# Key/value projections as seven block products (Strassen–Winograd) instead of eight

## The reference, cut to what matters

```python
q = rms_norm((x @ Wq).reshape(b, 32, 32, 128))
k = rms_norm((ctx @ Wk).reshape(b, 512, 8, 128))      # ctx is the same for both layers
v = (ctx @ Wv).reshape(b, 512, 8, 128)
probs = softmax(q @ k.T / sqrt(128))                  # 4 query heads share a key head
out = (probs @ v).reshape(b, 32, 4096) @ Wo
```

## Time and profile before

| | value |
|---|---|
| runs | 1511.18 us median, 1509.8 to 1514.25 |
| profiled execution: span | 1508.9 us; the median of the runs is 2.3 us above it |
| PE busy | 99% |
| DVE, ACT, POOL busy | 58%, 49%, 21% |
| granted TensorE clock | 0.999 of 2.4 GHz |
| chain that ended last | PE 94%, DVE 3%, ACT 1%, issue 1% |
| DMA | 99.37 MB, 66 GB/s on the mean |

### The profile page before, as it was taken

The page is one execution under the profiler, slowest core; times in us unless marked ns, Lnnn a source line. Parts: engine busy times, 40 slices in busy tenths (PEclk is TensorE's granted clock), DMA queues, the critical chain, the costliest instruction groups (busy, mean ns, idle before and its releaser), DMA issues.

```text
span 1508.9 us, 23714 instructions
## 1 busy us (share of the span) xinstructions
PE 1490.3 (99%) x8326; PEld 1269.7 (84%) x8326; DVE 876.7 (58%) x1645; ACT 733.5 (49%) x1360; POOL 311.5 (21%) x494
## 2 busy tenths in 40 slices
PE   8999999999999999999999999999999999999998
PEld 6888888888888888889778888888888888887887
DVE  6845554555555455758667555455554545577665
ACT  5634444545445454646456444444444444563443
POOL 2322221212222121014233222212222222101000
PEclk9999999999999999999999999999999999999999
DMA  8110000000000001447071000000000000252242
GB/s 326 53 66 30 17 27 19 19 26 12 35 16 26 19 20 62 147 170 258 29 279 60 22 8 28 7 21 21 7 28 7 21 14 15 93 187 91 85 167 98
DMA packets 29306, 99.37 MB, mean 66 GB/s; under 512 B 7040, under 2 KB 7808, under 8 KB 23648
## 3 DMA queue, kind: packets, MB, share of 16 engines
q1 hardware_dynamic: 29248, 98.60, 18.3%
HBM read 95.83 MB, written 2.75 MB: 65 GB/s over the span
## 4 chain that ended last, share of the span: by engine, by line
PE 94%; DVE 3%; ACT 1%; issue 1%; POOL 0%; DMA 0%; SPq 0%; DVEq 0%; POOLq 0%; ACTq 0%
PE g_kbanks L54 10%; PE g_kbanks L56 10%; PE g_kbanks L55 10%; PE g_vbank L54 9%; PE g_vbank L55 9%; PE g_vbank L56 9%; PE g_pobanks L1490 7%; PE g_pobanks L1478 4%; PE g_ktbank L1502 4%; PE g_sbank L1468 3%; PE g_sbank L54 2%; PE g_sbank L56 2%; PE g_sbank L55 2%; PE g_pobanks L54 1%; PE g_pobanks L56 1%; PE g_pobanks L55 1%
## 5 line engine op out<-in xcount | busy, mean ns | idle before, releaser
L54 PE MATMUL g_kbanks<-c_wkv_lo_r,c_cT_hi 128*128 128x512 f32 x640 | 262.5, 410 | 1.9 <-DVE c_wkv_lo_r L339 1.0
L56 PE MATMUL g_kbanks<-c_wkv_hi,c_cT_lo_r 128*128 128x512 f32 x640 | 250.4, 391 | 0.0
L55 PE MATMUL g_kbanks<-c_wkv_hi,c_cT_hi 128*128 128x512 f32 x640 | 249.8, 390 | 0.0
L54 PE MATMUL g_vbank<-c_wkv_lo_r,c_cT_hi 128*128 128x512 f32 x512 | 200.4, 391 | 0.0
L55 PE MATMUL g_vbank<-c_wkv_hi,c_cT_hi 128*128 128x512 f32 x512 | 200.0, 391 | 0.0
L56 PE MATMUL g_vbank<-c_wkv_hi,c_cT_lo_r 128*128 128x512 f32 x512 | 199.8, 390 | 0.0
L56 PEld LDWEIGHTS g_kbanks<-c_wkv_hi,c_cT_lo_r 128*128 128x128 f32 x640 | 120.1, 188 | 26.4
L54 PEld LDWEIGHTS g_kbanks<-c_wkv_lo_r,c_cT_hi 128*128 128x128 f32 x640 | 120.5, 188 | 24.7 <-issue 3.8
L55 PEld LDWEIGHTS g_kbanks<-c_wkv_hi,c_cT_hi 128*128 128x128 f32 x640 | 120.8, 189 | 20.7
L56 PEld LDWEIGHTS g_vbank<-c_wkv_hi,c_cT_lo_r 128*128 128x128 f32 x512 | 96.1, 188 | 20.6
L54 PEld LDWEIGHTS g_vbank<-c_wkv_lo_r,c_cT_hi 128*128 128x128 f32 x512 | 96.2, 188 | 18.5
(11 more groups left out here) (538 smaller groups left out, 3562.1 us busy)
## 6 DMA issues: line engine op xcount, KB each, us to landing
c_cT_lo<-in_ctx SPq DMA_DIRECT2D x64, 256.0 KB, 2.5
c_wkv_lo<-in_l_wo SPq DMA_DIRECT2D x16, 1024.0 KB, 4.8
g_stage<-in_l_wq SPq DMA_DIRECT2D x15, 1024.0 KB, 5.2
e_stage<-in_e_w SPq DMA_DIRECT2D x20, 768.0 KB, 4.1
c_wkv_lo<-in_l_wkv SPq DMA_DIRECT2D x8, 1024.0 KB, 7.5
m_stage<-in_mix_ffn SPq DMA_DIRECT2D x10, 768.0 KB, 4.6
c_vlat<-vlat_dram SPq DMA_DIRECT2D x32, 64.0 KB, 1.8
m_tw_lo<-in_mix_out SPq DMA_DIRECT2D x1, 1792.0 KB, 7.2
```

The source lines that it names most:

```text
L54: nc.tensor.matmul(out, a[0], b[1], start=start, stop=False)
L55: nc.tensor.matmul(out, a[0], b[0], start=False, stop=False)
L56: return nc.tensor.matmul(out, a[1], b[0], start=False, stop=stop)
```

## The change

Two key tiles and both columns (K and V) make a 2×2 block problem with an inner size cut in two: context blocks A11, A12, A21, A22 and weight blocks B11, B12, B21, B22. It was eight block products (48 matmuls for two key tiles); now seven (42), by sums of blocks made before. A product is 6 matmuls. The loop body is a **quad**: two key tiles, of which there are 32 in a layer, numbered m.

What goes with it:
- **Order of units**: all batches with the first half of heads, then all batches with the second, since seven weight blocks of one half fill the room. Halfway the weights are "turned": 4 POOL differences, 7 ACT and 7 DVE splits of 1024 columns (`turned_sum`, `turned_hi`, `turned_lo`).
- **Context blocks**: seven per pair of tiles, S1 to S4 made by POOL (4 operations of 256 columns), split by ACT and DVE in two pieces (768 and 1024 columns). This is done once, in the first half of the first layer. Each result (1.8 MB) is stored to DRAM, and fetched from there in all later units (48 fetches of 1.8 MB in two pieces).
- **Results**: the seven products end in two key banks and the value bank; ACT copies P1, P1-side partial sums (U2, U3) out, and DVE adds three times per quad.
- **Latents** of the first layer pass through the stream of query weights; their keys go through DRAM.
- The probabilities' 32 extra rows move from the score bank to the transpose bank.
- In the last quad two pieces of the output and four of the output weights are split.

```diff
-def mm3(nc, out, a, b, start, stop):
+def mm3(nc, out, a, b, start, stop, reopen=False):
...
+        def product(side, left, right, bank, start):
+            a, wt = context.block(side, left), kvw.block(right)
+            for c in range(DC // 2):
+                last = mm3(nc, bank[:, :], tuple(h[:, c * P:(c + 1) * P] for h in a),
+                           tuple(h[:, c * UW:(c + 1) * UW] for h in wt),
+                           start and c == 0, c == DC // 2 - 1, not start)
+            return last
...
+        def quad(hf, b, par, cycle, u, side, m):          # PE
...
+            need(pe, ka_added, m)
+            product(side, context.A11, kvw.B11, x_bank, True).then_inc(products, 1)
+            need(pe, k_normed, 2 * m)
+            product(side, context.A12, kvw.B21, y_bank, True).then_inc(products, 1)
+            if lags(u, side):
+                pv(a - 1, 1 - par if side else par, (2 * side - 1) % UNIT_H)
+            kt(2 * m - 1, 1, a if on else 0)
+            pe.wait_ge(p1_kept, m + 1)
+            product(side, context.S2, kvw.T2, x_bank, False).then_inc(products, 1)
+            need(pe, va_added, m)
+            product(side, context.S1, kvw.T1, zbank, True).then_inc(products, 1)
+            score(a, 1 - par, 2 * side)
+            pe.wait_ge(u2_kept, m + 1)
+            product(side, context.S3, kvw.T3, x_bank, False).then_inc(products, 1)
+            kt(2 * m, 0, a)
+            score(a + 1, 1 - par, 2 * side + 1)
+            pe.wait_ge(u3_kept, m + 1)
+            product(side, context.A22, kvw.T4, x_bank, False).then_inc(products, 1)
+            p_transpose(a, 2 * side, 2 * m + 1)
+            pe.wait_ge(vb_added, m + 1)
+            product(side, context.S4, kvw.B22, zbank, False).then_inc(products, 1)
+            pv(a, 1 - par, 2 * side)
+            p_transpose(a + 1, 2 * side + 1, 2 * m + 1)
...
+        def quad(hf, b, par, cycle, u, side, m):          # POOL
+            if prepared(hf, m + 1):
+                context.sums(pool, *following(hf, b, side))
+            if side == 1:
+                split_queries(u, par, 2 * m)
+            else:
+                root(2 * m, 0)
+            if is_at(m, PAIRS // 2 - 1):
+                pool.wait_ge(products, made(m, "p5"))
+                kvw.turned_sum(pool, 0)
+                pool.wait_ge(products, made(m, "p6"))
+                kvw.turned_sum(pool, 1)
+                pool.wait_ge(products, made(m, "p4"))
+                kvw.turned_sum(pool, 2)
+            root(2 * m + 1, 1)
+            if is_at(m, PAIRS // 2 - 1):
+                kvw.turned_sum(pool, 3)
```

More of the change, by code:

```diff
@@ L387, in product @@
         for h in range(GROUP):
-            last = mm3(self.nc, self.ybank[t], tuple(half[:, q % self.RING, h * P:(h + 1) * P] for half in self.split),
+            last = mm3(self.nc, self.ybank[t],
+                       tuple(self.context.slot(half, q % self.RING)[:, h * P:(h + 1) * P] for half in range(2)),
                        tuple(half[:, h * D:(h + 1) * D] for half in wt),
@@ L533, in gpsimd @@
                                     ALU.pow).then_inc(rstd_ready, 1)
+            if n in SUM_AT:
+                kvw.first_sum(pool, SUM_AT.index(n))
+            if NL and n == CTX_SUM_AT:
+                context.sums(pool, 0, 0)
+        for n in range(NN, OUTPUTS):
+            if n in SUM_AT:
+                kvw.first_sum(pool, SUM_AT.index(n))
     def tensor(pe):
@@ L1572, in finish @@
-            out.product(pe, 2 * UNIT_H + 1)
-            for q in range(2 * UNIT_H + 2, PARTS):
-                out.product(pe, q)
-                if after is not None and q == PARTS - 2:
+                score(a, 1, j)
+                if j:
+                    pv(a - 1, 1, j - 1)
+                out.product(pe, 2 * j + 2)
+                p_transpose(a, j, 2 * m)
+                out.product(pe, 2 * j + 3)
+            pv(LAST + UNIT_H - 1, 1, UNIT_H - 1)
+            for i in range(2 * UNIT_H + 2, PARTS):
+                out.product(pe, i)
+                if after is not None and i == PARTS - 2:
@@ new lines, in finish @@
+        def finish():
+            m = PAIRS
+            tail_heads(LAST - 1, UNIT_H - 1)
+            place_k(2 * m - 1, CT - 1, 1, UNITS - 1)
+            out.make_hi(act, 2)
+            for i in range(4, 6):
+                wo.make_hi(act, i)
+            for j in range(UNIT_H):
+                exponential(LAST + j, j)
+                divide(LAST + j, j)
+                out.make_hi(act, 2 * j + 3)
+                tail_heads(LAST + j, j)
+                out.make_hi(act, 2 * j + 4)
+                for i in range(2 * j + 6, 2 * j + 8):
+                    wo.make_hi(act, i)
+                if after is not None and j == 1:
+                    act.wait_ge(products, made(PAIRS - 1, "p3"))
+                    after.kv_split_hi(act)
+            out.make_hi(act, 11)
+            for i in range(14, 16):
+                wo.make_hi(act, i)
+            out.make_hi(act, 12)
+            for i in range(12, PARTS):
+                if i + 1 < PARTS:
+                    out.make_hi(act, i + 1)
@@ L1792, in finish @@
[L1792 to L1796 removed]
+                if after is not None and j == 1:
+                    after.kv_split_lo(dve)
+            out.make_lo(dve, 11)
+            for i in range(14, 16):
+                wo.make_lo(dve, i)
+            ot_place(LAST + UNIT_H - 1, UNITS - 1, UNIT_H - 1)
+            out.make_lo(dve, 12)
@@ L1797, in finish @@
+            for i in range(12, PARTS):
+                if i + 1 < PARTS:
+                    out.make_lo(dve, i + 1)
+                if after is not None and i < PARTS - 1:
+                    after.wide_lo(dve, i - 12)
                 if then:
-                    then[0].early_lo(dve, q - 12)
+                    then[0].early_lo(dve, i - 12)
             out.add(dve, 0)
```

1117 lines of the change are left out of this document (651 added, 466 removed).

## The result

The changed kernel takes 1548.5 us (median of 4 runs, 1547.3 to 1550.4) against 1510.5 us for the kernel before in the same comparison: 1.0249 times, 95% interval 1.0235 to 1.0264. It is slower. The forecast was 1514 us in a range of 1450 to 1550, with slower as the likeliest sign (0.46). The sign is right. That the time lies inside the range, by 1.5 us, is luck: the forecast's own mechanism reached to 1532, and the upper end was put there for rival 2, which did not come.

The account below looks back on a forecast made before the run. PE, busy 99%, bounds the kernel before; after the change a ring of waits sets the quad. Terms −10.8 − 6.8 + 2.0 − 3.4 + 16 + 6 = +3.0 us gave 1514 us, range 1450 to 1550.

Parts of the forecast that it names:

- rival 2: Each of 14 hand-offs between engines in a quad costs 0.05 us more: 1556 us, chance 0.12.
- The direct gain: On PE, 64 quads each with 6 matmuls less, 1.37 us per quad: 88 us.
- The floor: Quad time if PE stayed without gaps: 15.1 us in the first layer, 14.5 us in the second.
- The ring: Waits through PE, DVE, ACT and POOL from one quad's first score to the next's: 16.1 us first layer, 15.5 second.
- The turning: Weight change halfway through each layer delays the multiplication that P2 waits for: +8 us per layer, +16 in all.
- the third rival: DVE and POOL wait for each other in first-half quads (+10 us) and the turning (+2 per layer): 1528 us, chance 0.16.
- The first quads: First unit of each layer, without heads: two quads of 11.0 us replace four tiles of 5.9, −1.7 us per layer.
- Stores and fetches: Context blocks to and from DRAM, 1.8 MB per quad at some 118 GB/s with a quad of slack: 0 us.
- The last quads and the rest: Output-weight splits on DVE in the last quad, +3 us per layer; queries, output projection and small blocks, 0.
- PE as the bound: Ring shorter than added, so PE runs nearly without gaps at 14.6 us per quad: 1451 us, chance 0.24.
- Dearer hand-offs: Each of the ring's 14 hand-offs costs 0.05 us more, a quad 0.7: 1556 us, chance 0.12.
- DVE and POOL in turns: DVE operations with two SBUF inputs and POOL work lock each other out, in first-half quads and turning: 1528 us, chance 0.16.

Follow-up runs that it names:

- experiment 1: Changed kernel with ACT placing the next key copy before it divides the first head's scores: 1539.6 us.
- experiment 10: Changed kernel with DVE multiplying the keys by a constant, not waiting for POOL's root, so keys are not normalised: 1535.4 us.
- experiment 11: Experiment 7 plus POOL's root before its third sum, B22's low part before the copy of Pᵀ, and the queries' low part behind the second root: 1518.4 us.
- experiment 3: Changed kernel without loads, sums and splits of the second half's weights; products stay and use the first half's weights: 1521.9 us.
- Experiment 7: Experiment 1 plus DVE context work in idle stretches, turned splits spread over two quads, and the last quad's first output-weight splits later: 1530.9 us.

## Why the prediction was right in its sign and 34 us too low

**The direct gain.** Right in size (384 matmuls fewer), and no use by itself.

**The floor.** Right within 0.1: 14.5 forecast, 14.6 us for layer 2 (14.98 less the 0.38 that the wait costs, experiment 1). The expectation of experiment 10 takes it for 14.8, from the listed idle time alone. The quads did not reach it: even in experiment 11 they take 14.92 with the wait still there.

**The ring.** Its sums were right: 16.50 / 16.06 / 15.41 measured against 16.65 / 16.1 / 15.5, and PE's waits stand at the two places named, P2 and the first key transposes. The steps, too, are those of the chain that ended last in the changed kernel. Its reading as one ring was only half right. If it had been alone, experiment 1 would have given 0.62 us per quad and experiment 10 more; they gave 0 to 0.27 and 0 to 0.2. Three bounds of nearly the same length lie side by side: the ring through divide and root; maximum before multiplication on DVE against one product on PE; and in the first half DVE's context work. I had taken the second for a place at which the ring shows, and the third for a small term inside the ring (+0.15). That my sum met all three stretches within 0.15 us owes something to their lying so close together.

**The turning.** The dearest place, and a term that was too small: +8 per layer forecast, +12.5 and +11.6 measured, and experiment 3 shows it is the weights. The path was the forecast's: three sums, root, fourth sum, two ACT splits, last DVE split, multiplication, P2. P2 to P2 is 367.59 − 340.10 = 27.5 us where the forecast had 16.5 + 7.9 = 24.4. Of these 3.1 us, 2.9 are (a) POOL's instructions on this path, lengthened beside DVE's splits: two sums by 0.95 and 1.01, the power by 0.95. From there to the next P2 it is 385.32 − 367.59 = 17.7 us where a steady quad has 16.1. That fits (b) the clock, which was 0.50 until 371: 3.5 us of work at half speed lose some 1.7, an estimate. Neither was in the sum, and (a) had been put into the third rival at 2 us a layer.

The five splits also take 8.04 us where five of 1.22 that overlap by 0.1 make 5.7, but this was not on the path. The third of them met the fourth sum, and the last two had to wait for ACT's splits behind that sum in any case (361.17 + 3.36 = 364.53; ACT's first is done at some 364.5). Alone:

```profile
360.96 2.49 POOL L206 TENSOR_TENSOR c_wkv<-c_wkv 128x1024 f32<-128x1024 f32 x1
361.17 3.36 DVE L212 TENSOR_TENSOR c_wkv_r<-c_wkv,c_wkv_r 128x1024 fp32r<-128x1024 f32 x1
...
363.48 2.00 ACT L209 ACTIVATE c_wkv_r<-c_wkv 128x1024 fp32r<-128x1024 f32 x2 [3.60 <-POOL c_wkv L206]
```

**The first quads.** −1.7 per layer forecast, +6.5 and +1.1 measured. Four products of layer 1's first quad wait 0.47 to 0.78 us each, for copies of ACT and an addition of DVE, and P2 of the next 1.12; I had allowed 0.4 us a quad. In layer 1 POOL's sums wait 6.88 us for a context block whose load stands behind a store, and ACT, which waits for the sums, holds back the copy of U3 that PE needs:

```profile
113.95 3.14 POOL L396 TENSOR_TENSOR c_cT<-c_cT 128x256 f32<-128x256 f32 x4 [6.88 <-DMA c_cT<-in_ctx]
...
116.32 1.86 ACT L404 ACTIVATE c_cT_r<-c_cT 128x768 fp32r<-128x768 f32 x2 [3.84 <-POOL c_cT L396]
118.09 0.58 ACT L1899 ACTIVATE c0a_v<-g_kbanks 128x512 f32<-128x512 f32 x1
...
118.72 0.80 PE L54 MATMUL g_kbanks<-c_wkv_r,c_cT_r 128*128 128x512 f32 x1 [4.08 <-ACT c0a_v L1899]
```

The granted clock was 0.66 from 118 to 123. Stores and fetches at nothing was thus wrong at this one place. No edit took this wait away, so its price is read from the trace only.

**The last quads and the rest.** +6 and 0 forecast, +21.0 measured with what stands ahead of layer 1. In the last quad of layer 1 PE waits 2.52 us and its clock is 0.82 from 622 to 630. PE's idle time from there to layer 2 grew from 5.8 to 12.7 us (234.3 − 221.6), and its busy time by 2.9. The other long new wait is 1.96 us at the transposes of the queries just ahead of layer 2's first quad (842.59). Experiment 7 moved the first wait and gained nothing. How the 21 us divide beyond these waits was not separated by any run, and their cause stays open.

**The rivals.** PE as the bound: refuted, since experiments 1, 10 and 11 shortened the quads without taking a matmul away. (Its terms add up to 1449 us, not 1451; nothing hangs on it.) Dearer hand-offs, 1556 us: near in time and wrong in mechanism, since the steady quads show no 0.05 per hand-off. DVE and POOL in turns, 1528 us: the mechanism is real, but not where I had put it. In all 13 quads of the first half the low part of 1024 columns meets POOL's power, as foreseen, and neither is held up (1.21 to 1.22 and 1.01 to 1.02 us); the power had started 0.09 to 0.16 us earlier:

```profile
239.01 1.01 POOL L1611 TENSOR_TENSOR c0a_rstd<-c0a_ms,c_const 128x4 f32<-128x4 f32 x1
239.17 1.22 DVE L410 TENSOR_TENSOR c_cT_r<-c_cT,c_cT_r 128x1024 fp32r<-128x1024 f32 x1
```

At the turning the split had started first, by 0.13 us, and the power took 1.96. DVE's multiplication with two SBUF inputs is held up beside POOL's low part of the queries:

```profile
247.81 1.29 POOL L1625 TENSOR_TENSOR c0a_q_lo<-c_qT,c0a_q_hi 128x512 fp32r<-128x512 f32 x1
...
248.55 1.10 DVE L2012 TENSOR_TENSOR c0a_kn<-c0a_kn,c0a_rstd 128x512 f32<-128x512 f32 x1
```

POOL's low part keeps its 1.29 and ends at 249.10; the multiplication, with 0.69 in experiment 11, ends 0.55 later and has lost 0.41 us. The Trainium skill's "SBUF — State Buffer" (SBUF: two separate sides) says that such a pair of operations lock each other out for the whole instruction. The trace agrees for this pair and at the turning (0.41 us lost here), and not for the power and the split of the 13 quads, where the measurement decides. I had placed it in those 13 quads and the turning; it was in the turning and in every second quad, through the queries' low part, whose new neighbour the change had made: the first multiplication reads SBUF now, where before it read PSUM.

The sum of the errors: steady −0.5, first quads +11.0, turnings +8.1, last quads and rest +15.0, together +33.6 us, which is 36.6 measured less 3.0 forecast.

## What to carry to other kernels

When a kernel has one engine at 99% and the change shortens that engine's steps, add up not one ring but every list between two of its steps, and write down the second longest as well: it says what an edit to the longest is worth. Price what happens once (first quads, a change of weights, the last quad) by its own chain of waits: 25 us for two turnings outweighed the 16 us that all steady quads together had gained. A wait listed as 0.17 us cost 0.38: measure it by the distance between starts. An edit that shows nothing may be hidden behind an equal wait; try it again after that one is gone.
